# Narrow attentions that project for two tiles at a time instead of four

## What is computed

```python
def attention(q, k, v, mask):
    scores = jnp.einsum('bhqd,bhkd->bhqk', q, k) / jnp.sqrt(jnp.float32(HD))
    scores = scores * mask - 10000.0 * (1.0 - mask)
    probs = jax.nn.softmax(scores, axis=-1)
    return jnp.einsum('bhqk,bhkd->bhqd', probs, v)
ln_out = layernorm(hidden_states, ln1_s, ln1_b)
q, k, v = jnp.split(ln_out @ w_qkv + b_qkv, 3, axis=-1)
x = hidden_states + merge_heads(attention(split_heads(q), split_heads(k), split_heads(v), ltor_mask)) @ w_ao + b_ao
...
q, (k, v) = ln_out @ w_q + b_q, jnp.split(encoder_states @ w_kv + b_kv, 2, axis=-1)
```

## Time and profile before

| | us |
|---|---|
| median of 3 runs (1987.0 to 1987.67) | 1987.26 |
| the profiled execution | 1983.13 |
| its span | 1981.4 |
| layer 0: two wide attentions and the MLP | 0 to about 1248 |
| l1a, first projection to last output | 1261 to 1427 |
| layer 2 and the norm behind layer 1 | 1427 to 1553 |
| l3a1, first projection to last output | 1575.6 to 1699 |
| l3a2, the same | 1721.7 to 1845 |

### The profile page before, as it was taken

One profiled execution on the slowest core, in us unless ns is written; L12 is line 12 of the kernel. 1 busy time (PEld: TensorE's weight loads), 2 busy tenths in 40 slices (PEclk: granted clock), 3 DMA queues, 4 the chain that ended last, 5 costly groups with the idle time before them and its releaser, 6 DMA issues. The chain is left out here.

```text
span 1981.4 us, 37238 instructions
## 1 busy us (share of the span) xinstructions
PE 1752.4 (88%) x14606; PEld 1494.6 (75%) x14606; DVE 1046.4 (53%) x2150; ACT 990.5 (50%) x1858; POOL 530.0 (27%) x527
## 2 busy tenths in 40 slices
PE   5999999999969999999999689799769699698597
PEld 4988888888858888988889578576546467577486
DVE  5444444444464444444444733577689657666633
ACT  4444444444424444444444344466547577476443
POOL 5111111121121111111121210244430277377300
PEclk7999999999979999999999799899879799799799
DMA  4000000000020000000000100100100000100101
GB/s 150 23 22 21 0 21 21 21 19 2 1 65 22 22 7 14 21 21 21 0 21 1 46 0 0 27 1 2 39 14 0 25 1 2 36 2 1 46 0 43
DMA packets 55051, 39.80 MB, mean 20 GB/s; under 512 B 11891, under 2 KB 54450, under 8 KB 54962
## 3 DMA queue, kind: packets, MB, share of 16 engines
q1 hardware_dynamic: 54962, 38.57, 6.5%
HBM read 36.46 MB, written 2.10 MB: 19 GB/s over the span
## 5 line engine op out<-in xcount | busy, mean ns | idle before, releaser
L490 POOL TENSOR_TENSOR l0a_weight<-l0a_expd,l0a_inverse 64x256 f32<-64x256 f32 x128 | 103.6, 809 | 679.6 <-DVE l0a_inverse L686 678.5
L681 DVE TENSOR_TENSOR l0a_c_lo<-l0a_c_ps,l0a_c_hi 128x512 fp32r<-128x512 f32 x128 | 88.6, 692 | 307.4 <-ACT l0a_c_hi L636 307.4
L626 ACT ACTIVATE l0a_weight_t<-l0a_t_ps 128x512 f32<-128x512 f32 x128 | 76.6, 599 | 278.6 <-PE l0a_t_ps L532 278.6
L721 DVE TENSOR_TENSOR x<-l0a_o_ps,x 128x1024 f32<-128x1024 f32 x64 | 78.4, 1225 | 177.1 <-PE l0a_o_ps L101 177.1
L549 PEld LDWEIGHTS l0a_c_ps<-l0a_weight_t,l0a_v 128*128 128x128 f32 x1024 | 135.1, 193 | 13.5 <-ACT l0a_weight_t L626 2.3
L99 PE MATMUL l0a_o_ps<-l0a_wo_hi,l0a_c_hi 128*128 128x256 f32 x512 | 144.2, 282 | 0.0
L100 PE MATMUL l0a_o_ps<-l0a_wo_lo,l0a_c_hi 128*128 128x256 f32 x512 | 143.8, 281 | 0.0
L101 PE MATMUL l0a_o_ps<-l0a_wo_hi,l0a_c_lo 128*128 128x256 f32 x512 | 143.7, 281 | 0.0
L101 PE MATMUL l0a_v_ps<-l0a_wv_hi,ctx_lo 128*128 128x256 f32 x512 | 143.6, 280 | 0.0
L99 PE MATMUL l0a_v_ps<-l0a_wv_hi,ctx_hi 128*128 128x256 f32 x512 | 143.6, 280 | 0.0
L100 PE MATMUL l0a_v_ps<-l0a_wv_lo,ctx_hi 128*128 128x256 f32 x512 | 143.0, 279 | 0.0
(11 more groups left out here) (427 smaller groups left out, 4997.6 us busy)
## 6 DMA issues: line engine op xcount, KB each, us to landing
l0a_raw<-in_L_xattn_wq_dram SPq DMA_DIRECT2D x32, 128.0 KB, 2.3
l0a_raw<-in_L_xattn_wk_dram SPq DMA_DIRECT2D x32, 128.0 KB, 2.3
l0a_raw_v<-in_L_xattn_wv_dram SPq DMA_DIRECT2D x16, 256.0 KB, 3.1
l0a_raw_o<-in_L_xattn_wo_dram SPq DMA_DIRECT2D x32, 128.0 KB, 2.7
l0a_wo_all<-in_L_xattn_wo_dram SPq DMA_DIRECT2D x2, 2048.0 KB, 8.2
ctx_rows<-in_ctx_dram SPq DMA_DIRECT2D x4, 512.0 KB, 5.6
x<-in_x_dram SPq DMA_DIRECT2D x4, 512.0 KB, 8.7
l0m_raw<-in_L_xattn_w_fc_dram SPq DMA_DIRECT2D x2, 1024.0 KB, 5.5
```

What stands on the lines that cost most here:

```text
L490: pool.tensor_tensor(weight[SEQ:P, :, SEQ:P], expd[SEQ:P, :, 0:SEQ], inverse[SEQ:P].rearrange("p (t a) -> p t a", a=1) .to_broadcast([SEQ, ...
L626: act.activation(weight_t[:], t_ps[:], ACT.Copy).then_inc(t_done, 1)
L681: dve.tensor_tensor(c[p][1][:], c_ps[:], c[p][0][:].bitcast(F32), ALU.subtract).then_inc(c_lo, 1)
L721: dve.tensor_tensor(chip.x[:, rows, :], o_ps[:], chip.x[:, rows, :], ALU.add).then_inc(added, 1)
```

## The change

Queries and keys are made for a **unit** of two tiles (UT = 2, 256 rows). A product of one block is six matmuls of 256 columns; two blocks lie side by side in one bank. In l3a a unit is two slots: the even one projects both key blocks of the next unit (12 matmuls), the odd one both query blocks (12), and the eight copies are two in the even slot and six in the odd one. In l1a a unit is four slots: keys (6 matmuls) in slot 0, queries (12) in slot 2, copies three, two and three in slots 1, 2 and 3. Values are made for a pair of tiles in the first slot of a unit, and taken out by four copies of twice the size. q, kc and kb are half as large, and vb has room for six tiles. In a slot of ScalarE the spread copies now stand last. Ahead of the slots all keys go to bank_a and all queries to bank_b, and VectorE makes its copies before it takes the queries. CROSSED_CONTEXT is False, so what hangs on it does nothing. Since a line is inserted near the top, line numbers grow by 1, and by up to 19 further down.

```diff
--- before.py
+++ after.py
@@ narrow_attention: the tables @@
-    VR = 4
+    VR = 6
...
+    UT = 2
+    UN = UT * P
+    UNITS = NT // UT
...
-    GS = GT * CT
+    GS = UT * CT
     if CT == 2:
-        JOBS = {1: ("k", 0), 3: ("q", 0), 5: ("q", 1)}
-        SPREAD = {2: (0,), 3: (1, 2), 4: (3,), 5: (4, 5), 6: (6,), 7: (7,)}
+        JOBS = {0: "k", 2: "q"}
+        SPREAD = {1: (0, 1, 2), 2: (3, 4), 3: (5, 6, 7)}
     else:
-        JOBS = {0: ("k", 0), 1: ("k", 1), 2: ("q", 0), 3: ("q", 1)}
-        SPREAD = {1: (0, 1), 2: (2, 3, 4), 3: (5, 6, 7)}
+        JOBS = {0: "k", 1: "q"}
+        SPREAD = {0: (0, 1), 1: (2, 3, 4, 5, 6, 7)}
...
+    def value_pair(s):
+
+        return s // (2 * CT) if s < CHUNKS and s % (2 * CT) == 0 else None
...
-        q = [sb(f"q{b}", [P, QB, GN]) for b in range(2)]
-        kc = sb("kc", [P, KB, GN])
-        kb = [sb(f"kb{b}", [P, KB, GT * HB, PER, SEQ]) for b in range(2)]
+        q = [sb(f"q{b}", [P, QB, UN]) for b in range(2)]
+        kc = sb("kc", [P, KB, UN])
+        kb = [sb(f"kb{b}", [P, KB, UT * HB, PER, SEQ]) for b in range(2)]
@@ TensorE @@
-                def project(out, what, x, g):
-                    tokens = slice(g * GN, (g + 1) * GN)
+                def project(out, what, g):
+                    tokens = slice(g * UN, (g + 1) * UN)
                     src, w_ = (chip_h, wq) if what == "q" else (source, wk)
...
+                    for x in range(QB if what == "q" else KB):
+                        feats = slice(x * P, (x + 1) * P)
+                        for c in range(CH):
+                            last = product(pe, out[:, x * UN:(x + 1) * UN], w_[0][:, c, feats], w_[1][:, c, feats],
+                                           src[0][:, c, tokens], src[1][:, c, tokens], start=c == 0, stop=c == CH - 1)
...
-                    g, i = t // GT, t % GT
+                    g, i = t // UT, t % UT
                     if s % GS == 0:
-                        pe.wait_ge(q_taken, (g + 1) * QB)
+                        pe.wait_ge(q_taken, g + 1)
                         pe.wait_ge(parts_act, parts_by_act(g))
...
-                            pe.wait_ge(value_taken, min(NT, (s + CT - 1) // CT))
+                            pe.wait_ge(value_taken, pairs_before(s))
...
-                for n, (what, x) in enumerate([("k", x) for x in range(KB)] + [("q", x) for x in range(QB)]):
...
+                project(bank_a, "k", 0)
+                project(bank_b, "q", 0)
@@ ScalarE @@
-                    for b in range(HB):
-                        src = bank_a[b * SEQ:(b + 1) * SEQ, 0:VC].rearrange("p (h j f) -> p j h f", j=2, f=HD)
...
+                    for a in range(2):
+                        src = bank_a[a * SEQ:(a + 1) * SEQ, 0:2 * VC].rearrange("p (n h j f) -> p j n h f", n=2, j=2, f=HD)
...
-                    parts, g = spread_of(s)
-                    for m in parts:
-                        spread(m, g)
-                    if multiply and value_tile(s) is not None:
-                        take_values(value_tile(s))
-                    if 0 <= s - 1 < CHUNKS:
-                        exponent(s - 1)
...
+                    if multiply and value_pair(s) is not None:
+                        take_values(value_pair(s))
+                    if 0 <= s - 1 < CHUNKS:
+                        exponent(s - 1)
...
+                    if job is not None and job[0] == "k":
+                        take_keys(bank_b, job[1])
                     parts, g = spread_of(s)
                     for m in parts:
                         spread(m, g)
@@ VectorE @@
+                    for x in range(QB):
+                        last = dve.tensor_scalar(q[g % 2][:, x, :], src[:, x * UN:(x + 1) * UN], bias_cols[:, BQ + x:BQ + x + 1],
+                                                 None, ALU.add)
...
+                dve.wait_ge(k_taken, 1)
                 for m in FIRST_DVE:
...
+                take_queries(bank_b, 0)
```

More of the change, by code:

```diff
@@ L28 @@
 HB = P // SEQ
+CROSSED_CONTEXT = False
 class Chip:
@@ L1134, in made_before @@
         def made_before(what, s):
-            return (QB if what == "q" else KB) + sum(1 for i in range(s) if (j := job_of(i)) and j[0] == what)
+            return 1 + sum(1 for i in range(s) if (j := job_of(i)) and j[0] == what)
         def part(m, g, engine_in):
@@ L1162, in _ @@
                         shift(s - 1)
-                    if value_tile(s) is not None:
-                        add_bias(value_tile(s))
+                    if tile_start(s) is not None:
+                        add_bias(tile_start(s))
                     if s < CHUNKS:
@@ L1172, in _, with values @@
             def _(pe):
-                def project(out, what, x, g):
-                    tokens = slice(g * GN, (g + 1) * GN)
+                def project(out, what, g):
+                    tokens = slice(g * UN, (g + 1) * UN)
                     src, w_ = (chip_h, wq) if what == "q" else (source, wk)
[L1176 to L1179, removed]
-                    last.then_inc(q_made if what == "q" else k_made, 1)
[L1182 to L1186, removed]
+                    for x in range(QB if what == "q" else KB):
[3 more added lines that the diff above has]
+                                           src[0][:, c, tokens], src[1][:, c, tokens], start=c == 0, stop=c == CH - 1)
+                    last.then_inc(q_made if what == "q" else k_made, 1)
+                def values(m):
+                    for n in range(2):
+                        tok = slice((2 * m + n) * P, (2 * m + n + 1) * P)
+                        for c in range(CH):
+                            last = product(pe, bank_a[:, n * VC:(n + 1) * VC], source[0][:, c, tok], source[1][:, c, tok],
+                                           wv[0][:, c, :], wv[1][:, c, :], start=c == 0, stop=c == CH - 1)
                     last.then_inc(value_made, 1)
@@ L1273, in _ @@
                         turn_rows(done)
-                    if value_tile(s) is not None:
+                    if value_pair(s) is not None:
                         if c >= 0:
@@ L1295, in _, with take_keys @@
             def _(act):
-                def take_keys(src, x, n):
-                    act.wait_ge(k_made, n)
-                    act.activation(kc[:, x, :], src[:], ACT.Identity, bias=bias_cols[:, BK + x:BK + x + 1]).then_inc(k_taken, 1)
+                def take_keys(src, g):
+                    act.wait_ge(k_made, g + 1)
+                    for x in range(KB):
+                        last = act.activation(kc[:, x, :], src[:, x * UN:(x + 1) * UN], ACT.Identity, bias=bias_cols[:, BK + x:BK + x + 1])
+                    last.then_inc(k_taken, 1)
                 def spread(m, g):
-                    act.wait_ge(k_taken, g * KB + m // PER + 1)
+                    act.wait_ge(k_taken, g + 1)
                     out, in_, own = part(m, g, kc)
@@ L1327, in exponent @@
                     act.activation(score[c % LAG][:], score[c % LAG][:], ACT.Exp).then_inc(exp_done, 1)
[L1329 to L1333, removed]
+                take_keys(bank_a, 0)
+                for m in FIRST_ACT:
+                    spread(m, 0)
                 for s in range(SLOTS):
@@ L1400, in add_output @@
                     measure(chip, dve, t)
-                for n, (what, x) in enumerate([("k", x) for x in range(KB)] + [("q", x) for x in range(QB)]):
-                    if what == "q":
-                        take_queries(banks[n % 2], x, 0)
+                dve.wait_ge(k_taken, 1)
                 for m in FIRST_DVE:
-                    dve.wait_ge(k_taken, m // PER + 1)
                     out, in_, own = part(m, 0, kc)
                     dve.tensor_scalar(out, in_, own, None, ALU.mult).then_inc(parts_dve, 1)
+                take_queries(bank_b, 0)
                 for s in range(SLOTS):
```

50 lines of the change are left out of this document (25 added, 25 removed).

## The result

The changed kernel takes 1993.52 us (median of 7, 1992.21 to 1995.06), beside 1986.59 (1983.93 to 1987.67) for the kernel before: a ratio of 1.0037, 95% interval 1.0025 to 1.0048, **0.37% slower**. The forecast was 1994.7. The profiled execution took 1993.5 us (span 1991.8), 10.4 more than the one shown of before.

The account below looks back on a forecast made before the run. Bound: in l3a PE and the VectorE-GpSimd loop, within 0.1 us of each other; in l1a PE. Two l3a stages +6.0 and l1a +1.4 make +7.4 on 1987.26: 1994.7 us, 8 in 10 from 1981 to 2001.

Parts of the forecast that it names:

- The stall in l3a: l3a's odd slots: six copies behind the exponent hold the next scores 1.45 us; a unit takes 14.0 us, not 12.67.
- Chunk 4 to 12: l3a's steady stretch: four units, each 1.33 us longer, add 5.3 us a stage.
- the tail: l3a's last three tops, chunk 12 to 15: 18.8 us again, a change of 0.
- Rival (b): l3a: VectorE and GpSimd set the tops up to slot 8, two units pay, not four: 1989 us, chance 0.17.
- The start of l3a: First matmul to first scores falls from 9.86 to 6.0 us: gain 3.8 us (3.3 to 4.3), twice.
- The entry: l3a's slots before slot 5: the top of chunk 4 falls 1.5 us later against the first scores (0 to 3).
- PE's projections: Twelve matmuls of 256 columns take some 1.52 us (upper bound 1.60); PE pays 0.0 to 0.1 us a block pair.
- rival (d): l3a and l1a: matmuls of 256 columns cost 1.5 times their share, +12 us: 2006 us, chance 0.02.
- The value copies: l3a's even slot: four double-size copies at 0.4 us each ahead of the exponent, just covered by PE's attend and output.
- rival (c): Value copies of 0.55 to 0.6 us not covered, keys 0.6 us late in five units, +6: 2000 us, chance 0.14.
- l1a: Layer 1 stage: start gains 3.6 us, slots lose 5.0 with units of 19.5 us; together +1.4 us (-1.5 to +3).
- The clearing: GpSimd's clearing of the larger vb, some 1 us longer in l3a, costs nothing.

Follow-up runs that it names:

- The run with the copies ahead: Changed kernel with ScalarE's six copies in l3a's odd slots moved ahead of the exponent: 1984.92 us, ratio 0.9996 against before.
- the runs of one stage at a time: Kernel before with only layer 3's change: 1994.47 us (ratio 1.0048); with only layer 1's attention changed: 1982.47 us (0.9985).
- four and four: Changed kernel with two of l3a's six odd-slot copies moved to the end of the even slot: 1990.18 us.
- all three edits: Changed kernel with l3a's copies and keys ahead of the exponent and l1a's queries ahead of the top: 1973.94 us, ratio 0.9937 against before.

## Why the prediction was right, and where it was lucky

- **The stall in l3a, right in place and sum, wrong in its parts.** Copies from T + 4.29, scores at T + 7.84 (forecast 7.95), a unit of 13.97 (14.0). The end of the copies sets this, so PE's own work, put at 12.6 by taking one whole value product out of a 6.32 us slot, could be wrong by 0.3 without the sum noticing. The run with the copies ahead put it at 12.90: a burst of matmuls has its slower first step in the odd slot too, and the transposes wait a tenth for weights and keys. So the stall is 1.07 us and not 1.45, and even without it PE needs 0.23 us a unit more than the 12.67 of before.
- **Chunk 4 to 12** +5.2 (forecast +5.3), **the tail** 0.0 (0). Rival (b), the late stall, is out: the scores wait from chunk 6 on.
- **The start of l3a** 6.43 us in place of 6.0, a gain of 3.4 (3.8); in l3a2 6.14, a gain of 4.0. Keys and copies came as forecast; the queries' projection, still at the low clock, was later by 0.55, the wait in DVE's row.
- **The entry** +2.4 (forecast +1.5, 0 to 3). The forecast followed the scores forward, not ScalarE: the keys of slot 2 stand behind an exponent that waits for GpSimd, and bank_b for them, 1.32 us in slot 3. With the copies ahead of the exponent the entry is +1.0, with the keys ahead of it too -0.6, so both held it. With these terms a stage is -3.4 + 2.4 + 5.2 = +4.1 (by the unrounded times) in l3a1, +3.5 in l3a2, where +3.0 was forecast.
- **PE's projections** right: twelve matmuls of 256 columns take 1.53 us (1627.51 to 1629.04), forecast 1.52, and 1.62 in the odd slot, where they start the burst, just above the bound of 1.60; rival (d) is out, and with it the line that the prediction drew between two spacings of the Trainium skill: these twelve are 0.12 us apart, not 0.098.
- **The value copies** 389 ns each (forecast 0.4), covered; rival (c) is out. (Its sign, transposes into bank_b that wait for keys, did appear, but once a stage and from another cause, under the entry.)
- **l1a, wrong.** The unit (19.5) and the start (5.14, forecast 5.0) were right. The first queries hold bank_b for 2.70 us, not 0.8, since VectorE has masked scores and tops to do ahead of them. From chunk 3 to 31 it took 132.65 us and not 134.7: the wait comes ahead of chunk 3's masked scores, so the first unit behind them took 18.33 us, where the sum had 19.5 and 0.8 for the wait. Against the same execution of before the whole stage is therefore 0.0 and not +1.4. The larger error is the yardstick: the earlier trace rows are from an execution in which the old start went better than in the two other traced ones. Against those the change is worth -2.5 by the traces, and -3.8 by the medians.
- **The clearing, wrong.** "GpSimd then stands 7.24 us before the slots begin: nothing" asked only whether GpSimd had time. It cost 1.8 us by the traces and 3.4 by the medians, since VectorE stands meanwhile.

So the forecast of 1994.7 was right in its main mechanism, and close in number by luck: by the traces l3a was 1.6 us worse than forecast (+7.6), its setups 1.8 (forecast 0), and l1a 3.9 better (-2.5), and these errors nearly cancelled. The three parts come to the +6.9 of the medians, which is luck as well, since the runs of one stage at a time give other sizes.

## What to carry to other kernels

Work that the next step of another engine needs must not stand behind an instruction that waits: here six copies of 2.5 us cost no wait ahead of the exponent and cost 1.1 us a unit behind it, and moving three things forward in their queues turned a loss of 0.37% into a gain of 0.63%. Ask of every operation that grows not only whether its own engine has time, but which other one stands while it runs. And before costing a start by one execution, look at its granted clock: the old l1a took 2.5 us more in two of three.

## What the runs showed of the hardware

TensorE's granted clock falls to half not only where TensorE does little (0.51 from 1427 to 1460 in before, with 6 us of work in 33), but in the first slots of a stage, where it works with gaps, and then the time that it stays there differs from run to run. The longest, in the profiled run with the copies ahead, most of it in the window 1282 to 1300:

```profile
1282.00:1300.00 18.00, 18.00 (x139) 13.44 (x138) 7.47 (x9) 7.34 (x15) 5.18 (x4) 0.50 0.00 1
```

Eighteen microseconds at 1.2 GHz with PE busy throughout; with the windows on either side it is near 24, from 1277.5 to 1301.4. The stage took 174.4 us where the others take 165.1, and this is the execution of 1993.35 us beside others of the same kernel at 1978. What had gone before was the wait for the queries in slot 3 (2.71 us). Five others with this l1a had the same wait (2.69 to 2.71): in four the clock was low for between 3 and 4 us behind it (0.88 in the window 1276 to 1290), in the fifth (four and four) not at all, and its stage took 163.6 us. So the wait doesn't decide alone. With all three edits, where the wait is 1.45 us, the five executions lie within 1.7 us (1973.13 to 1974.86). That the shorter gaps are why is not shown: too few executions have a trace, and the seven of the changed kernel, with the long wait, lie within 2.9 us.
